# The first two layers of a hybrid network: batch norm roots on two columns, residual in one operation, small work moved between engines

## The reference, cut to what matters

```python
# L0: attention over the image, with its own batch norm, and a residual
g_x   = maxpool2(conv1x1(x, Wg, bg));  phi_x = maxpool2(conv1x1(x, Wp, bp))
f     = einsum('bni,bim->bnm', theta_x, phi_x)
y     = einsum('bnm,bmi->bni', softmax(f), g_x)
w_y   = conv1x1(y, Ww, bw)
w_y   = (w_y - mu) * rsqrt(var + EPS) * gamma + beta        # mu, var over the batch
x1    = w_y + x
# L1: two binary convolutions, bn(x, g, b, m, v) = x * inv + (b - m * inv), inv = g * rsqrt(v + EPS)
out1 = conv3x3(sign(x1 + b11), mean|w3| * sign(w3))
out1 = prelu(x1 + bn(out1, g1, be1, m1, v1) + b12, a1) + b13
out2 = conv1x1(sign(out1 + b21), mean|w1| * sign(w1))
out2 = prelu(bn(out2, g2, be2, m2, v2) + out1 + b22, a2) + b23
# then layer norms, an 8-head attention, 8 gated experts, a second attention, 16 gated experts
```

## Time and profile before

| | us |
|---|---|
| median of 3 runs | 372.19 (372.12 to 373.61) |
| the profiled execution | 376.23 |
| its span | 374.4 |
| TensorE busy in the span | 334.3 (89%) |
| VectorE busy | 264.3 (71%) |
| ScalarE busy | 220.1 (59%) |
| GpSimd busy | 165.0 (44%) |

### The profile page before, as it was taken

How to read it: one execution, slowest core, us unless ns; L and a number is a source line. 1 busy time by engine, 2 the same in 40 slices (tenths; PEclk the granted TensorE clock), 3 DMA queues, 4 the chain that set the end, 5 groups by cost and what they waited for, 6 DMA issues and landing times.

```text
span 374.4 us, 6864 instructions
## 1 busy us (share of the span) xinstructions
PE 334.3 (89%) x2286; PEld 215.9 (58%) x2286; DVE 264.3 (71%) x678; ACT 220.1 (59%) x557; POOL 165.0 (44%) x178
## 2 busy tenths in 40 slices
PE   6995367999999999999788999869798999999996
PEld 5651246777777777667454433435265866666761
DVE  0788967888888888887553587787886844455551
ACT  1545449888888988889646663461225644444550
POOL 6000045755555555555500000050200799999994
PEclk9999556999999999999989999986999999999999
DMA  7926000000000000000000794000001965766521
GB/s 210 221 59 221 0 0 1 3 3 1 0 2 3 1 2 2 2 2 0 2 0 4 235 381 177 0 3 0 0 2 27 337 220 221 224 222 170 201 85 57
DMA packets 16275, 30.86 MB, mean 82 GB/s; under 512 B 5808, under 2 KB 9584, under 8 KB 16240
## 3 DMA queue, kind: packets, MB, share of 16 engines
q1 hardware_dynamic: 15776, 29.60, 24.7%
q10 hardware_dynamic: 464, 0.82, 1.0%
HBM read 29.70 MB, written 0.72 MB: 81 GB/s over the span
## 4 chain that ended last, share of the span: by engine, by line
PE 67%; DVE 15%; ACT 10%; issue 5%; DMA 1%; POOL 1%; SPq 0%; DVEq 0%; ACTq 0%; POOLq 0%
PE ps L1144 15%; PE ps L1152 8%; PE ps L945 7%; PE ps L975 6%; PE ps L957 6%; PE ps L1099 4%; PE ps L1092 4%; ACT va_vb L674 3%; PE ps L869 2%; PE ps L923 2%; DVE negmax L1714 2%; PE ps L1249 1%; PE ps L1048 1%; DMA x<-in_x 1%; PE ps L1003 1%
## 5 line engine op out<-in xcount | busy, mean ns | idle before, releaser
L534 POOL TENSOR_TENSOR va_vb<-va_vb,rowinv 128x512 f32<-128x512 f32 x64 | 66.5, 1040 | 57.1 <-DVE rowinv L1721 57.0
L674 ACT ACTIVATE va_vb<-ps,negmax 128x256 f32<-128x256 f32 x128 | 59.5, 470 | 10.0 <-DVE negmax L1714 9.2
L809 ACT ACTIVATE wy<-ps 128x512 f32<-128x512 f32 x64 | 38.1, 597 | 42.8 <-PE ps L1144 42.8
L1144 PE MATMUL ps<-XP,early 64*128 64x256 f32 x512 | 57.5, 379 | 0.0
L1144 PEld LDWEIGHTS ps<-XP,early 64*128 64x128 f32 x512 | 46.8, 186 | 12.4 <-issue 4.9
L945 PE MATMUL ps<-keys_gates,XX 128*128 128x512 f32 x128 | 48.0, 457 | 2.9 <-ACT va_vb L674 1.5
L1714 DVE TENSOR_REDUCE negmax<-ps 128x2 f32<-128x512 f32 x64 | 43.9, 687 | 1.6 <-PE ps L945 0.4
L957 PE MATMUL ps<-consts,va_vb 128*128 128x128 f32 x256 | 40.0, 279 | 4.4 <-POOL va_vb L534 2.9
L957 PEld LDWEIGHTS ps<-consts,va_vb 128*128 128x128 f32 x256 | 30.2, 149 | 12.3 <-POOL va_vb L534 6.3
L975 PE MATMUL ps<-pT,vproj 128*64 128x256 f32 x256 | 35.7, 388 | 0.0
L665 ACT ACTIVATE keys_gates<-ps 64x256 fp32r<-64x256 f32 x64 | 24.2, 377 | 9.8 <-PE ps L923 8.6
(11 more groups left out here) (323 smaller groups left out, 638.7 us busy)
## 6 DMA issues: line engine op xcount, KB each, us to landing
pT<-gates_row SPq DMA_DIRECT2D x16, 512.0 KB, 5.0
vproj<-gates_row SPq DMA_DIRECT2D x14, 512.0 KB, 5.4
gate_row_keys<-gates_row SPq DMA_DIRECT2D x14, 512.0 KB, 5.2
early<-in_f_in SPq DMA_DIRECT2D x1, 2048.0 KB, 8.3
consts<-in_consts SPq DMA_DIRECT2D x1, 813.0 KB, 5.7
x<-in_x SPq DMA_DIRECT2D x1, 512.0 KB, 5.3
w2raw<-in_f_in SPq DMA_DIRECT2D x1, 512.0 KB, 6.7
out<-in_f_out SPq DMA_DIRECT2D x1, 512.0 KB
```

What stands on the lines that cost most here:

```text
L534: gp.tensor_tensor(prob[:, n % 4], prob[:, n % 4], rowinv[:, n % 4, :].unsqueeze(2).broadcast_to([P, U, N]), ALU.mult).then_inc(S("p_scale ...
L674: ins = act.activation(prob[:, n % 4, h, :], ps[:, 1 + n % 2, h * N:(h + 1) * N], ACT.Exp, bias=negmax[:, n % 4, h:h + 1], accum_out=rowsu ...
L809: act.activation(act_out[:, kk % 2, :].rearrange("p (o n) -> p o n", o=2), ps[:, 2 * pair_of(kk):2 * pair_of(kk) + 2, 0:2 * P], ACT.Silu). ...
L1144: mm = pe.matmul(ps[:, 2 * pair_of(kk) + o, w * 2 * P:(w + 1) * 2 * P], w3raw[r, e, w * HID:(w + 1) * HID], pairs(c, 2)[r], start=True, st ...
```

## The change

It has these parts: the order of `VECS` puts g1 and g2, be1 and be2, m1 and m2, v1 and v2, b12 and b22 side by side, so that `v_both` can address two columns; epsilon is added to v1 and v2 at the start of VectorE's list; ScalarE copies gw; the root of the stored variances becomes an instruction of its own, placed ahead of the evictions of wy; the sum over |w3| moves ahead of the softmax; x1 is made without the shift in one operation, and the shift goes into the bias of the sign (column 40) and into the bias of what is added to the convolution (column 41); the second norms' small work is done on two columns; the fillers before the convolution fall from 8 to 3.

```diff
-VECS = ["bpg", "bt", "bw", "gamma", "beta", "b11", "b12", "b13", "b21", "b22", "b23",
-        "g1", "be1", "m1", "v1", "g2", "be2", "m2", "v2", "a1", "a2"]
+VECS = ["bpg", "bt", "bw", "gamma", "beta", "b11", "b12", "b22", "b13", "b21", "b23",
+        "g1", "g2", "be1", "be2", "m1", "m2", "v1", "v2", "a1", "a2"]
...
+        def v_both(name):
+
+            return vec[:, VI[name]:VI[name] + 2]
...
+            act.wait_ge(S("blocks_zeroed"), 2)
+            act.wait_ge(S("gw_done"), 1)
+            for g in range(G):
+                h = slice(C * g, C * g + C)
+                act.activation(gw[h, :, g, :], ps[h, 4, :].rearrange("p (j g c) -> p j g c", g=G, c=C)[:, :, g, :],
+                               ACT.Copy).then_inc(S("gw_evac"), 1)
...
+            act.wait_ge(S("bn_var_ready"), 1)
+            act.activation(col[:, 12:14], col[:, 9:11], ACT.Sqrt).then_inc(S("bn_std_ready"), 1)
             for p in range(2):
                 act.wait_ge(S("wy_counted"), p + 1)
...
-            act.wait_ge(S("bn_var_ready"), 1)
-            act.activation(col[:, 11:14], col[:, 8:11], ACT.Sqrt).then_inc(S("bn_std_ready"), 1)
-            act.wait_ge(S("bn_scale_ready"), 1)
-            act.activation(va[:, 512:1024], wy[:, 512:1024], ACT.Identity, scale=col[:, 28:29],
-                           bias=col[:, 29:30]).then_inc(S("va_act"), 1)
+            act.wait_ge(S("bn_var_ready"), 2)
+            act.activation(col[:, 11:12], col[:, 8:9], ACT.Sqrt).then_inc(S("bn_std_ready"), 1)
...
-                               ACT.Sign, bias=v_("b11")).then_inc(S("sgn_ready"), 1)
+                               ACT.Sign, bias=col[:, 40:41]).then_inc(S("sgn_ready"), 1)
...
-            keep_clock(pe, 2, 8)
+            keep_clock(pe, 2, 3)
...
+            dve.wait_ge(S("vec_loaded"), 16)
+            ts(col[:, 9:11], v_both("v1"), EPS_BN, None, ALU.add).then_inc(S("bn_var_ready"), 1)
...
+            dve.wait_ge(S("l1_loaded"), 80)
+            dve.tensor_reduce(col[:, 20:21], w3n[:], AX.X, ALU.add, apply_absolute_value=True)
...
-            dve.wait_ge(S("gw_done"), 1)
-            for g in range(G):
-                h = slice(C * g, C * g + C)
-                dve.tensor_copy(gw[h, :, g, :], ps[h, 4, :].rearrange("p (j g c) -> p j g c", g=G, c=C)[:, :, g, :]
-                                ).then_inc(S("gw_evac"), 1)
...
-            step(ts(col[:, 9:10], v_("v1"), EPS_BN, None, ALU.add))
-            step(ts(col[:, 10:11], v_("v2"), EPS_BN, None, ALU.add))
...
-            step(dve.reciprocal(col[:, 24:27], col[:, 11:14]))
+            step(dve.reciprocal(col[:, 25:27], col[:, 12:14]))
+            inv, low, shift = col[:, 32:34], col[:, 38:40], col[:, 29:30]
+            step(tt(inv, v_both("g1"), col[:, 25:27], ALU.mult))
+            dve.wait_ge(S("bn_std_ready"), 2)
+            step(dve.reciprocal(col[:, 24:25], col[:, 11:12]))
...
+            step(tt(shift, v_("beta"), col[:, 30:31], ALU.subtract))
+            tt(col[:, 40:41], shift, v_("b11"), ALU.add)
             dve.wait_ge(S("l0_loaded"), 32)
             for p in range(2):
+                dve.wait_ge(S("wy_evac"), p + 1)
                 s = slice(p * 512, (p + 1) * 512)
-                if p == 0:
-                    step(ts(va[:, s], wy[:, s], col[:, 28:29], col[:, 29:30], ALU.mult, ALU.add))
-                else:
-                    dve.wait_ge(S("va_act"), 1)
-                tt(x1[:, s], va[:, s], x0[:, s], ALU.add).then_inc(S("x1_ready"), 1)
...
+                stt(x1[:, s], wy[:, s], col[:, 28:29], x0[:, s], ALU.mult, ALU.add).then_inc(S("x1_ready"), 1)
+
+            tt(col[:, 34:36], inv, col[:, 22:24], ALU.mult)
+            step(tt(low, inv, v_both("m1"), ALU.mult))
+            step(tt(low, v_both("be1"), low, ALU.subtract))
+            step(tt(col[:, 36:38], low, v_both("b12"), ALU.add))
+            step(tt(col[:, 41:42], col[:, 36:37], shift, ALU.add))
...
+            dve.wait_ge(S("x1_ready"), 2)
+            for p in range(2):
+                ins = ts(half_of(va, p), half_of(x1, p), col[:, 41:42], None, ALU.add)
+            step(ins)
 
             dve.wait_ge(S("fold_high"), 2)
             tt(GG[C:P], ps[C:P, 3, :], GG[C:P].bitcast(F32), ALU.subtract).then_inc(S("fold_split"), 1)
```

More of the change, by code:

```diff
@@ L1509, in _ @@
             step(ins)
-            dve.wait_ge(S("vec_loaded"), 16)
             dve.wait_ge(S("blocks_zeroed"), 2)
@@ L1537, in _ @@
                 tt(f_prob[:, q], f_exp[:, q], wide(f_col[:, 2, q], t=8), ALU.mult).then_inc(S("f_prob_ready"), 1)
-            dve.wait_ge(S("l1_loaded"), 80)
-            ones = [("w3n", w3n, 9 * C, 20), ("w1n", w1n, C, 21)]
-            for _, w, n, c in ones:
-                step(dve.tensor_reduce(col[:, c:c + 1], w[:], AX.X, ALU.add, apply_absolute_value=True))
-            step(ts(col[:, 22:23], col[:, 20:21], 1.0 / (9 * C), None, ALU.mult))
-            step(ts(col[:, 23:24], col[:, 21:22], 1.0 / C, None, ALU.mult))
+            step(dve.tensor_reduce(col[:, 21:22], w1n[:], AX.X, ALU.add, apply_absolute_value=True))
+            ts(col[:, 22:23], col[:, 20:21], 1.0 / (9 * C), None, ALU.mult)
+            ts(col[:, 23:24], col[:, 21:22], 1.0 / C, None, ALU.mult)
             dve.wait_ge(S("f_transposed"), 2)
@@ L1567, in _ @@
             ts(col[:, 8:9], col[:, 4:5], EPS_BN, None, ALU.add).then_inc(S("bn_var_ready"), 1)
-            step(tt(col[:, 2:3], ps[:, 6, 0:1], v_("bw"), ALU.add))
+            tt(col[:, 2:3], ps[:, 6, 0:1], v_("bw"), ALU.add)
             dve.wait_ge(S("bn_std_ready"), 1)
-            step(dve.reciprocal(col[:, 24:27], col[:, 11:14]))
+            step(dve.reciprocal(col[:, 25:27], col[:, 12:14]))
+            inv, low, shift = col[:, 32:34], col[:, 38:40], col[:, 29:30]
+            step(tt(inv, v_both("g1"), col[:, 25:27], ALU.mult))
@@ L1586, in _ @@
-            for k, (g_, be, m_, b_) in enumerate((("g1", "be1", "m1", "b12"), ("g2", "be2", "m2", "b22"))):
-                inv = col[:, 32 + k:33 + k]
-                step(tt(inv, v_(g_), col[:, 25 + k:26 + k], ALU.mult))
-                step(tt(col[:, 34 + k:35 + k], inv, col[:, 22 + k:23 + k], ALU.mult))
-                step(tt(col[:, 38:39], inv, v_(m_), ALU.mult))
-                step(tt(col[:, 39:40], v_(be), col[:, 38:39], ALU.subtract))
-                step(tt(col[:, 36 + k:37 + k], col[:, 39:40], v_(b_), ALU.add))
+                stt(x1[:, s], wy[:, s], col[:, 28:29], x0[:, s], ALU.mult, ALU.add).then_inc(S("x1_ready"), 1)
@@ new lines, in _, with half_of @@
+            tt(col[:, 34:36], inv, col[:, 22:24], ALU.mult)
[3 more added lines that the diff above has]
+            step(tt(col[:, 41:42], col[:, 36:37], shift, ALU.add))
+            def half_of(a, p):
+                return a[:, p * 512:(p + 1) * 512]
+            dve.wait_ge(S("x1_ready"), 2)
+            for p in range(2):
+                ins = ts(half_of(va, p), half_of(x1, p), col[:, 41:42], None, ALU.add)
@@ L1595, in _ @@
+            step(ins)
             dve.wait_ge(S("fold_high"), 2)
             tt(GG[C:P], ps[C:P, 3, :], GG[C:P].bitcast(F32), ALU.subtract).then_inc(S("fold_split"), 1)
-            def half_of(a, p):
-                return a[:, p * 512:(p + 1) * 512]
             def norm_and_prelu(p, bank, ready, k, dst, a, after, done):
@@ L1610, in norm_and_prelu @@
                     ALU.add).then_inc(S(done), 1)
-            for p in range(2):
-                ins = ts(half_of(va, p), half_of(x1, p), col[:, 36:37], None, ALU.add)
-            step(ins)
             for p in range(2):
```

3 lines of the change are left out of this document (removed).

## The result

| | changed kernel | kernel before, same chip |
|---|---|---|
| median of 17 runs | 370.97 us (368.38 to 376.10) | 372.82 us (371.91 to 375.33) |
| ratio | 0.9928, 95% interval 0.9906 to 0.9951 | |
| the profiled execution | 376.10 us | 376.23 us |
| its span | 374.3 us | 374.4 us |

A forecast was written before the change was run, and what follows sets the result against it. The early chain of waits through VectorE and ScalarE, not TensorE, was taken as the bound. Running leads of 0.68, 1.19 (1.03 at the second statistics), 1.2, 1.63, 2.05 and 3.05 us gave 372.19 - 3.05 = 369.1 us; range 367.6 to 371.4.

The forecast's parts named there:

- 1. softmax sums: Softmax on VectorE: with the value copies moved to ScalarE, the sums start at 16.12, a lead of 0.68 us.
- 2. copy of the second half: Probabilities' second half on VectorE: with the w3n sum moved earlier, its copy starts near 19.83, a lead of 1.19 us.
- 3. variance (L1565, L1566): Second norms: epsilon additions move earlier, but L1565 waits for TensorE's joined mean; it starts at 23.49, lead 1.2 us.
- 5. convolution: Residual's first half, in one operation, ends 2.05 us earlier, so the convolution starts at 26.94 instead of 28.99.
- The price chosen for the residual: The residual's single scalar-tensor-tensor operation per half was taken to cost 0.75 us, with 0.65 as the lower bound.
- step 6: Between residual and convolution result: less small VectorE work, L1605 near 29.2, lead 3.05 us; the convolution is then late next.
- The cover is the same: Before the convolution: with three fillers TensorE idles 0.85 us against 0.79, so its clock was expected to hold.
- The rival that I gave 0.05: Convolution falls to the low clock with five fillers gone: 3.6 us more, lead gone, 372.7 us; chance 0.05.
- I carry 3.05 through: Behind the convolution, 32.27 to 50 us: same instructions on the same engines, so the whole 3.05 us lead was kept.
- ScalarE did not hold the first half: Rival in the softmax: sums start no earlier, the first two gains vanish, 2.0 us remain, 370.2 us; chance 0.10.
- step 4: ScalarE's root: table load moves to 19.82, behind the probabilities' copy and covered; reciprocal at 24.47, lead 1.63 us.
- the clock gives back a lead at its rise near 62 us: Rival: TensorE's clock rise stays put while work comes earlier, 2.0 us given back, 371.1 us; chance 0.15.

The follow-up runs named there:

- the softmax part alone: Kernel before with only gw copied by ScalarE, the w3n sum ahead of the row maxima and one wait less in the small column work: 371.23 us, ratio 0.9974.
- second trace of after: The changed kernel with the same code, run again on another occasion for a trace: 371.04 us, ratio 0.9949.
- before's second trace: The kernel before, unchanged, run once more for another trace: 372.52 us (one run).
- the norm part alone: Changed kernel with VectorE copying gw again and w3n summed behind the probabilities; three fillers stay: 371.46 us, ratio 0.9973.
- the version with the early weight loads: Changed kernel with w0 on its own semaphore, so ScalarE issues its weight loads without waiting for x; norms stated against the kernel before: 371.17 us, ratio 0.9957.

## Why the prediction was right, and where it was wrong

**The sum was right, term by term.** With eight fillers, counted from the score products (11.91 before, 11.35 here):

| event | before | eight fillers | lead | predicted |
|---|---|---|---|---|
| 1. softmax sums | 16.80: 4.89 | 15.53: 4.18 | 0.71 | 0.68 |
| 2. copy of the second half | 21.02: 9.11 | 19.18: 7.83 | 1.28 | 1.19 |
| 3. variance (L1565, L1566) | 24.70: 12.79 | 22.87: 11.52 | 1.27 | 1.2 |
| 4. reciprocal | 26.10: 14.19 | 23.83: 12.48 | 1.71 | 1.63 |
| 5. convolution | 28.99: 17.08 | 26.35: 15.00 | 2.08 | 2.05 |
| 6. its result taken (L1605, L1608) | 32.27: 20.36 | 28.58: 17.23 | 3.13 | 3.05 |

The column before is the earlier trace rows. The price chosen for the residual between 0.65 and 0.75 was the right one: two took 1.41. The two parts alone give 1.14 and 2.22, together 3.36 for 3.13 of both, so they are nearly additive; with both in, the convolution itself is the next limit, as step 6 said.

**The failing step is the last of the change: "The cover is the same".** The idle time was computed rightly (0.82 to 0.83 us for 0.85), but the conclusion, that the clock stays as it was with 0.79, does not follow from it. Before and with the softmax part alone, 0.79 and 0.80 us of idle time behind eight fillers did no harm in three traces; 0.82 and 0.83 behind three did in three of four; with no idle time that the profile shows, behind eight, none of the kernels fell. The rival that I gave 0.05 is what the three traces of the changed kernel show, and its price was wrong as well: I let the whole convolution run low (3.6 us more), but the clock came back within it, 5.73 to 5.84 for 4.22, so 1.6, and VectorE waited 1.52 to 1.62. The lead in the second and third trace is 1.61, not nothing. The Trainium skill, "TensorE: Matmul & The Clock Gate", Part 1, says that the gate's window runs freely, so that the same kernel changes level at different points in different runs; three falls and one cover at the same 0.82 to 0.83 us of idle time agree with that, and so do the places of the falls, from 0.20 us ahead of the convolution's start to 0.28 behind it. What I compared was the last gap alone. What stood ahead of it had changed too: 1.90 us of fillers had become 0.82. Which of the two decides no run here tells; what the runs show is that with five fillers more the clock held in five traces of five.

**A second loss was not foreseen:** the gap of 0.42 us behind the convolution. The sentence that failed is "From 32.27 to 50 both kernels have the same instructions on the same engines, so I carry 3.05 through": the instructions are the same, their starts are not. Of the lead of 3.13 it leaves 2.7, and of after's 1.61 it leaves 1.2 at the layer norm's transposes (44.16 - 10.03 = 34.13 in the second trace of after, 44.73 - 9.40 = 35.33 in the second of before).

**Why the time came out near the forecast all the same.** The traces of after lead by 1.2 us at the layer norm, but the medians of its three occasions say 1.9, 1.9 and 2.0 us (the ratios 2.7, 1.9 and 2.0). And with eight fillers, which lead by 2.7 there, median and ratio say 2.2. The 1.5 us between the traces of the two kernels show as 0.3 in the medians. Two things in the record bear on this.

The first is which executions the traces are of: the slowest of each occasion, with mean granted clocks of 0.936, 0.945 and 0.945, where the median of the changed kernel's 41 executions is 0.952. Sorted by the mean granted clock of the whole execution (the kernel before: its 75 executions beside the experiments):

| mean granted clock | changed kernel, mean time | kernel before, mean time |
|---|---|---|
| 0.963 | 368.86 us (6) | 372.48 us (14) |
| 0.954 | 370.36 us (11) | 373.54 us (33) |
| 0.945 | 373.21 us (7) | 373.45 us (4) |

At 0.963 the changed kernel gains 3.6 us and at 0.954 3.2, near the forecast; at 0.945, where two of its traces lie, 0.2. A mean does not say where in the execution the clock was low, so this is a hint and no proof that the executions without a fall gain about what was forecast.

The second is a step of 1.2 us much later. ScalarE's table loads mark stages; in before's second trace, in the second trace of after, and with eight fillers:

```profile
189.50 1.28 ACT L626 ACT_TABLE_LOAD   x1
196.15 1.28 ACT L639 ACT_TABLE_LOAD   x1
...
277.73 1.28 ACT L639 ACT_TABLE_LOAD   x1
```

```profile
188.77 1.28 ACT L630 ACT_TABLE_LOAD   x1
196.64 1.28 ACT L643 ACT_TABLE_LOAD   x1
```

```profile
276.84 1.28 ACT L643 ACT_TABLE_LOAD   x1
```

The same stage took 6.65 us in the one and 7.87 in the other, and in before's first trace it took 7.88. The busy tables name the cause, in before's second trace and in after's second:

```profile
190.00:192.00 2.00, 1.79 (x17) 0.93 (x13) 1.93 (x6) 0.79 (x1) 0.00 (x0) 1.00 0.00 0
```

```profile
190.00:192.00 2.00, 2.00 (x12) 0.92 (x9) 1.54 (x5) 0.05 (x1) 0.00 (x0) 0.50 0.00 0
```

It is the clock again. In all 13 traces the stage takes 6.63 to 6.65 us where the clock stays at 1.00 (eight traces) and 7.87 to 7.91 where it is at 0.50 in a part of it (five: before, the norm part alone, two of after, and the version with the early weight loads): not a matter of the change, but of the execution. With eight fillers the carry worked as predicted up to the gap: 276.84 - 11.35 = 265.49 against 277.73 - 9.40 = 268.33, a lead of 2.84 at 277 us, with the clock at 1.00 through that stage in both. The second trace of after, at 278.24, is 268.21 behind its score products, and before's first trace, which has the low clock in that stage too, 281.43 - 11.91 = 269.52: a lead of 1.31.

With such a step drawn anew in each execution, and score products that start anywhere from 8.98 to 11.91, twelve runs do not settle 1.5 us, and each ratio's interval is some 0.9 us to either side. So the forecast of 3.05 was near to the measured 1.9 to 2.7 partly by luck: the sum for a kernel with its clock held was right but for the gap (2.7 to 3.1), and the kernel run loses another 1.5 us wherever its clock falls ahead of the convolution. In what share of its executions that happens is left open. The upper part of the range, which holds 370.97, was there for a rival that did not occur.

**The other rivals.** ScalarE did not hold the first half: its two copies took 0.76 us together and its queue was idle for 1.25 ahead of the probabilities with eight fillers (0.4 each was my figure). The table load stood at 19.25 with eight fillers, with the root at 20.54 and the first eviction at 21.36, as step 4 had it. That the clock gives back a lead at its rise near 62 us is not what was seen: the rise came at 57.65 with eight fillers, 46.3 behind the score products, for 49.2 and 50.4 in the two traces of before, and the lead of eight fillers was 2.85 at the end of attention.

**Run time goes with the clock.** The changed kernel's first 17 runs go from 368.38 us, at a mean granted clock of 0.963, to 376.10, at 0.936. That is 7.7 us between executions of the same code, far more than the change is worth, and the reason why the profiled time of 376.10 says nothing against the median.

## What to carry to other kernels

Fillers that hold the clock belong to the price of the stage behind them: when a change shortens the wait in front of a stage, don't cut them by the sum of idle time, keep them running up to the stage, and look at the pass spacing in several traces, since one may show the good case. Look also at where the traced executions lie among the timed ones: three traces of slow executions do not tell how the median one ran. Compare traces from an event behind the first loads (here the score products repeated to 0.01 us), not from the start. And where an operation moves ahead of others on its engine, the load that it needs now holds those others too.

## What the runs showed of the hardware

- Three fillers ahead of the convolution with 0.82 to 0.83 us idle: 18 passes in 5.73 to 5.83 us in three of four traces, 4.22 in the fourth; with no filler and 1.58 idle 5.84; with eight and none idle 4.21 in all five traces.
- With 56 fillers more than the eight before the convolution, 23 of them ahead of the layer norm, the clock was at 1.00 from 5 to 240 us: a pair of score products (128x512) took 0.74 us there, 1.22 with the low clock. The medians, of two occasions, are 1.8 us apart (370.68 and 368.90).
- One stage near 190 us took 6.63 to 6.65 us in the eight traces whose clock stayed at 1.00 through it and 7.87 to 7.91 in the five in which it was at 0.50 for a part of it.
- The convolution's passes are as slow or as fast beside the same transfers: six in a microsecond at clock 1.00 and four at 0.50, with 386 GB/s moved in both (26 to 27 us of the norm part alone and of the second trace of after).
- Between VectorE's queue seeing its semaphore and the start of L1612, 0.46 to 0.48 us passed where 0.04 is usual, at one place only, in each of nine traces of the kernels with both parts. No view of the profile says why.
- A switch of ScalarE's table cost 1.28 us, and the next operation started right behind it (19.25, 20.54 with eight fillers): nothing more was seen on the engine on either side.
